# Third attention: the causal mask moves from a product on TensorE into the buffer of the relative-position term, and GpSimd's packing gets a second multiply

## What is computed

```python
q = _apply_rotary_interleave(q, cos, sin)
k = _apply_rotary_interleave(k, cos, sin)
q = q / sqrt(DIM_PER_HEAD)
scores = jnp.einsum('bhqd,bhkd->bhqk', q, k)
pos = jnp.arange(L)
rel_idx = jnp.clip(pos[None, :] - pos[:, None], -MAX_REL_POS, MAX_REL_POS) + MAX_REL_POS
rel = rel_emb[rel_idx]
scores = scores + jnp.einsum('bhqd,qkd->bhqk', q, rel)
causal = jnp.tril(jnp.ones((L, L), dtype=bool))
scores = jnp.where(causal[None, None], scores, NEG_INF)
attn = jax.nn.softmax(scores, axis=-1)
ctx = jnp.einsum('bhqk,bhkd->bhqd', attn, v)
ctx = ctx + jnp.einsum('bhqk,qkd->bhqd', attn, rel)
out = ctx.transpose(0, 2, 1, 3).reshape(B, L, MODEL_DIM) @ w_o.T
```

## Time and profile before

| | |
|---|---|
| median of 3 runs | 3445.43 us (3441.07 to 3450.32) |
| profiled execution | 3436.04 us, of which its span 3434.3 us |
| granted TensorE clock, mean over the span | 0.907 |
| PE busy | 2934.0 us, 85% |
| DVE busy | 2324.1 us, 68% |
| ACT busy | 1501.0 us, 44% |
| POOL busy | 1276.9 us, 37% |

### The profile page before, as it was taken

One profiled execution on the slowest core, in us unless ns is written; L12 is line 12 of the kernel. 1 busy time (PEld: TensorE's weight loads), 2 busy tenths in 40 slices (PEclk: granted clock), 3 DMA queues, 4 the chain that ended last, 5 costly groups with the idle time before them and its releaser, 6 DMA issues. The chain is left out here.

```text
span 3434.3 us, 42926 instructions
## 1 busy us (share of the span) xinstructions
PE 2934.0 (85%) x16742; PEld 1788.1 (52%) x16742; DVE 2324.1 (68%) x3225; ACT 1501.0 (44%) x2848; POOL 1276.9 (37%) x1083
## 2 busy tenths in 40 slices
PE   6989998799799995799978888768888989998589
PEld 3544555577444443577755556555553333334367
DVE  4444436699777512799968878469956757775688
ACT  1333333366266500466535555347753433432155
POOL 2322201266311000366546556147723434442054
PEclk8989988799899987899979989779998999999799
DMA  2000010233100100355422212224300000001032
GB/s 83 1 1 1 1 65 1 75 123 123 60 1 1 46 33 13 87 124 125 101 64 60 56 47 72 89 87 146 136 25 0 1 1 1 1 1 42 0 124 86
DMA packets 32718, 180.69 MB, mean 53 GB/s; under 512 B 7297, under 2 KB 7553, under 8 KB 16673
## 3 DMA queue, kind: packets, MB, share of 16 engines
q1 hardware_dynamic: 32514, 177.93, 16.8%
HBM read 161.33 MB, written 15.47 MB: 51 GB/s over the span
## 5 line engine op out<-in xcount | busy, mean ns | idle before, releaser
L302 PE MATMUL ps<-parts 128*128 128x512 f32 (+7 forms) x7520 | 1562.5, 413 | 168.8 <-DVE parts L316 72.8
L302 PEld LDWEIGHTS ps<-parts 128*128 128x128 f32 (+3 forms) x7520 | 1025.0, 190 | 747.8 <-issue 231.8
L316 POOL TENSOR_TENSOR work<-work 128x512 f32<-128x512 f32 x480 | 631.4, 1316 | 987.9 <-DMA work<-scr_w 489.3
L312 ACT ACTIVATE work<-ps 128x512 f32<-128x512 f32 (+4 forms) x898 | 523.0, 608 | 579.6 <-PE ps L302 562.4
L316 DVE TENSOR_TENSOR parts<-work,parts 128x512 fp32r<-128x512 f32 x468 | 652.0, 1404 | 35.0 <-ACT parts L312 34.0
L332 DVE TENSOR_REDUCE fw_sb<-ps 128x2 f32<-128x1024 f32 (+3 forms) x384 | 415.0, 1086 | 274.7 <-PE ps L302 274.0
L302 PE MATMUL ps<-work 128*32 128x256 f32 (+5 forms) x2396 | 366.2, 422 | 36.1 <-DMA work<-work 27.6
L312 ACT ACTIVATE parts<-work 128x512 fp32r<-128x512 f32 x468 | 294.7, 631 | 187.7 <-DVE work L316 172.8
L312 ACT ACTIVATE fw_sb<-ps 128x512 f32<-128x512 f32 (+5 forms) x394 | 204.6, 536 | 311.6 <-PE ps L302 266.6
L306 PE MATMUL ps<-wc_sb,fw_sb 128*128 128x128 f32 x1128 | 211.9, 300 | 35.7 <-DVE work L335 11.7
L302 PEld LDWEIGHTS ps<-work 128*32 128x32 f32 (+2 forms) x2396 | 138.7, 137 | 198.7 <-issue 135.8
(11 more groups left out here) (124 smaller groups left out, 2991.4 us busy)
## 6 DMA issues: line engine op xcount, KB each, us to landing
work<-scr_w SPq DMA_DIRECT2D x74, 1024.0 KB, 4.7
work<-scr_w SPq DMA_DIRECT2D x72, 512.0 KB, 6.4
work<-scr_sk SPq DMA_DIRECT2D x64, 128.0 KB, 2.6
scr_sp<-wr_sb SPq DMA_DIRECT2D x64, 128.0 KB, 2.2
fw_sb<-in_f SPq DMA_DIRECT2D x1, 6528.0 KB, 18.6
fw_sb<-in_f SPq DMA_DIRECT2D x1, 5376.0 KB, 15.6
fw_sb<-in_f SPq DMA_DIRECT2D x1, 4608.0 KB, 18.6
scr_sk<-work SPq DMA_DIRECT2D x64, 64.0 KB, 1.7
```

Source lines behind the costliest of these rows:

```text
L302: return self.e.matmul(o, l, r, start=start, stop=stop) if self.e else Unwritten()
L312: return self.e.activation(o, i, f, bias=bias, scale=scale)
L316: return self.e.tensor_tensor(o, a, b, op) if self.e else Unwritten()
```

## The change

The product with the mask tile goes, so the score product is the only one of its bank. The mask is held in `BT` instead. There the key columns behind a strip's own 32 keys are filled with NEG (-1.0e30), and within the strip's diagonal block the skew memory supplies it: `begin_dve` builds in `PW` 512 zero columns and 512 columns with a 32 x 32 diagonal block of the mask, each value for 16 heads, and `begin_sp` writes that into both `sk` buffers in place of zeros. The skewed writes of the learned term overwrite it left of the diagonal and on it only. POOL's first write to `PW` waits for these DMAs. POOL's pack multiplies by the reciprocal, as before, and then by the constant 1.0 in the same instruction.

```diff
                 ins = self.scores_pe(e, i, X, n)
-                if self.causal:
-                    ins = e.matmul(X[:, n - 128:n], k.idb[:, :], k.cmb[:, :], start=False)
                 ins.then_inc(*k.summed.up((t, "scores", i)))
...
-        return e.matmul(X[:, 0:n], R(self.Qz[b, qt, g][:, tile(j)]), R(self.K[b][:, g * 512:g * 512 + n]), stop=False)
+        return e.matmul(X[:, 0:n], R(self.Qz[b, qt, g][:, tile(j)]), R(self.K[b][:, g * 512:g * 512 + n]))
...
     def begin_dve(self, e):
         k, t = self.k, self.t
+        e.memset(self.PW[:, 0:512], 0.0).then_inc(*k.made_v.up((t, "before diagonal")))
+        for u in range(4):
+            r = slice(32 * u, 32 * u + 32)
+            e.copy(view(self.PW[r, 512:1024], [16, 32], [1, 16]), view(k.cm[r, r], [1, 32], [0, 16])
+                   ).then_inc(*k.made_v.up((t, "diagonal", u)))
         for i in range(2):
-            e.memset(self.BT[i], 0.0).then_inc(*k.made_v.up((t, "clear band", i)))
+            for u in range(4):
+                c = 512 * u + 1024
+                e.memset(self.BT[i][32 * u:32 * u + 32, 0:c], 0.0).then_inc(*k.made_v.up((t, "clear band", i, u)))
+                if u < 3:
+                    e.memset(self.BT[i][32 * u:32 * u + 32, c:2560], NEG).then_inc(*k.made_v.up((t, "later keys", i, u)))
...
     def begin_sp(self, e):
         k, t = self.k, self.t
-        e.wait_ge(*k.made_v[t, "clear band", 0])
+        e.wait_ge(*k.made_v[t, "diagonal", 3])
         for i in range(2):
-            e.dma_start(self.sk[i], self.BT[0][:, 0:1024]).then_inc(*self.cleared.up(i))
+            e.dma_start(self.sk[i], self.PW[:, 0:1024]).then_inc(*self.cleared.up(i))
...
-        e.wait_ge(*k.made_v[t, "clear band", 1])
+        e.wait_ge(*k.made_v[t, "clear band", 1, 3])
...
+        e.wait_ge(*self.cleared[1])
         if qt == 0 and g == 0:
             e.memset(self.PW[:, 0:512], 0.0).then_inc(*k.made_g.up((t, "no key", b)))
...
-            e.ts(view(self.PW[:, 16 * lo + h:16 * lo + h + 1], [16, n]), a.P[u][:, c:c + n], a.acc[b, qt][:, x:x + 1], ALU.mult
+            e.ts(view(self.PW[:, 16 * lo + h:16 * lo + h + 1], [16, n]), a.P[u][:, c:c + n], a.acc[b, qt][:, x:x + 1], ALU.mult, 1.0, ALU.mult
                  ).then_inc(*k.made_g.up((t, "packed", u)))
```

## The result

The changed kernel took 3464.3 us (median of 4 runs, 3456.59 to 3468.40) against 3444.9 us (4 runs, 3441.07 to 3450.32) for the kernel before. The ratio is 1.0056, interval 1.0034 to 1.0079: slower by 19 us, between 12 and 27. Timed once more beside other kernels it gave 1.0046, 1.0032 to 1.0060, that is 16 us (11 to 21). The forecast was 3457, slower, with 3441 to 3490 as its range.

The account below looks back on a forecast made before the run. DVE holds up the start; in the loop POOL, a ring of four engines or DVE sets the pace by query tile. +18.4 (start) - 7 (masks) + 0 (second multiply) = +11.4 us on 3445.43, so 3457, range 3441 to 3490.

Parts of the forecast that it names:

- The start: Stage start: 15872 added fill columns on DVE and four diagonal copies lengthen the path by 18.4 us, bounds 18.0 and 20.5.
- PE's 25 us: Stage start, profile after: PE would stand idle about 25 us while DVE fills and copies.
- the time of SP's DMAs: Stage start: SP's two skew-memory DMAs, now behind the fourth diagonal copy, come about 3.3 us after 1724.68, at the same time.
- The masks: Loop: 68 of the 256 dropped mask products count, at 0.10 us each, so 7 us less, bounds 5 and 12.
- The half-way price: Mask products on PE: 0.10 us taken for each, from 0.07 to 0.15 us at 2.4 GHz.
- The second multiply: POOL's 256 packs: a second operation in the same instruction adds nothing, 0 us.
- a sign of being wrong: POOL's packs: the prediction is wrong if the spacing of the packs moves.
- rival B: POOL's packs get quicker, at the cast's pace, with DVE right behind: about -6 us, 3451; chance 0.11.
- Rival A: POOL's second multiply costs time: +17 us (3474) or +55 us (3512); chance 0.13 for each size.
- Rival C: PE sets the loop's pace, so all 256 masks count: 46 us go, 3418; chance 0.06.
- The last sign of being wrong: Loop: the prediction is wrong if a batch with query tile 2 or 3, held to be DVE's, gets shorter.
- a ring: Loop, query tile 1: four engines in a ring set the pace, a turn of 4.30 us, packs 2.96 of it.

Follow-up runs that it names:

- the short maximum: Kernel before with DVE's row maximum taken over the last 128 columns of each score row instead of all n: 3396.59 against 3441.17 us, ratio 0.9867.

## Why the prediction came out as it did

**The start: right in kind and place, 1 us too small.** It said +18.4, with bounds of 18.0 and 20.5, and nothing to hide it. DVE's part grew by 19.25 us, the kernel with the fills alone gave +19.6. That a fill on 32 rows costs what one on 128 costs held. The columns came dearer: the 20480 behind the copies took 22.3 us, 1.09 ns each instead of 1.04. That is 0.9 us more, some 0.07 us for each of the 14 strips, where 0.2 us had been put for all 13 added fills. The copies took 1.70 us as put. PE's 25 us and the time of SP's DMAs came as written; the first bias add stood 47.5 us behind the first fill, where 46.3 had been worked out. The stated upper bound has a slip: with 2.8 us for the copies the sum is 19.5, not 20.5. The 19.25 us of the profile lie inside it, the 19.6 of the fills alone just above.

**The masks: count right, price too high.** The term was 68 products at 0.10 us. The step measured here fell from 0.388 to 0.318 us, so a mask is worth 0.07, the lower bound. 68 x 0.07 = 4.8 us, and the kernel without masks gave -4.8; with 1 to 8 us as its interval the agreement to the tenth is chance, and that just these 68 masks count was not tested. The half-way price rested on the suspicion that the mask delays the load behind it, by comparison with products of another stage; the step from the score is 0.32 us without a mask as well, so that length is not the mask's doing. DVE's waits of over 0.15 us for PE, from the first to the last row maximum, fell from 50.0 us to 46.1 and 48.5 in two profiles of the changed kernel, and to 46.7 with the masks alone gone: by 2 to 4 us, not by 7.

**The second multiply: the number 0 held, its reason fell.** The forecast said that a pack's pace is set by something other than a multiply, such as its scattered writes, and so would not move. It moved by a third, down, which the forecast itself had named as a sign of being wrong. That the term of 0 still fits is luck. The shorter pack is rival B's mechanism, seen in the profile: packs of 0.54 us, a POOL round of 3.32 us where 3.5 was to stand. Its price was wrong too: it said -6, and the kernel with nothing but the second multiply gave 0, to 3 us either way. DVE stands closer behind POOL than B allowed: its 0.2 us in a batch does show in a single turn, but the 32 batches of query tiles 0 and 1 together took 2.3 us less in the changed kernel and 1.0 with the second multiply alone, not 6, though the four packs are about 0.9 and 1.2 us shorter in each. The exponentials' waits only change their source, from POOL to the row maximum. Rival A has the wrong sign altogether. By the Trainium skill (GPSIMD Engine Reference, section 7), at four cycles for each dependent step, the second multiply would have doubled the price; the runs show the reverse. By the Trainium skill (GPSIMD Engine Reference, section 3.1) a second operation is free; that comes nearer, but in this trace the pack got shorter, from 838 to 536 ns.

**The loop.** Rival C, PE as the pace, is out: 256 masks less gave 5 us, and 51 us less on DVE gave 46, with the open share of the clock said above. The last sign of being wrong didn't come: the batches with query tiles 2 and 3 took 98.9 and 153.8 us before and 100.5 and 155.2 in the changed kernel, not less. That DVE holds the pace was right for tile 2 and, going by the short maximum, only in part for tile 3. For tiles 0 and 1 the forecast gave the pace to POOL or to a ring, and there much shorter packs gave 2.3 us: DVE stands right behind.

**The sum.** By the measured terms it is 19.6 - 4.8 + 0 = +14.8 us, where 11.4 was forecast: 1.2 us more in the start, 2.2 in the masks, and a 0 in the packs that held by luck. The two comparisons gave +19.3 (12 to 27) and +15.8 (11 to 21). The 4.5 us between the sum and the first of them are inside the spread; no term was found for them. A single profile can't settle it, since the loop's length differs by several microseconds from one profiled execution to another: it was 418.3 us in that of the kernel with the second multiply alone, whose time over its runs didn't change.

## What to carry to other kernels

Before work is moved into a buffer's contents, count the columns that someone must write before the first use, and who stands behind that writer: here 16,000 columns on DVE cost four times what 256 small products on TensorE gave back, and the same contents written in fewer blocks by two engines that stood idle cost nothing. When two engines' waits alternate ahead of a third, shortening one of them shows nothing until the other is lightened: the packs gave 0 us at first and 13 us once DVE had less to do. The price of an operation with another form is read from a row of that form; one run with the forms side by side is cheap.

## What was unexpected of the hardware

- POOL's tensor-scalar with one operation is slower than with two. With outputs 16 words apart, 160 columns took 820 ns with one operation and 538 to 555 ns with two, and 128 columns 713 and 481 to 543. Start to start the packs take 0.71 and 0.60 us before, 0.43 and 0.37 after, which is about 3.3 and 1.7 ns for each further column.
- DVE's fills on 32 rows take as long as on 128: one of 2560 columns shows 2.19 us on both, with 0.59 us of idle time ahead on 32 rows and 0.48 on 128 that nothing released. A duration without the idle time in front understates such a fill by a fifth.
- ACT with a scale of zero and a bias fills about as quickly as DVE: 12 blocks with 8192 columns took 8.98 us, 1.10 ns per column, against DVE's 1.04 to 1.09.
- After 15.0 us without a product PE ran seven steps of the preparation at 0.72 us each, after 25.7 us the same seven at 0.42; the granted clock over these steps was 0.50 and 1.00. In the kernel with the fills alone, also after 25.7 us, the first of the seven took 0.72 and the others 0.42. What decided it is open.
